# A mixture-of-experts tail on one core: TensorE reads and checks the next block's expert number one block ahead, behind the row transposes

## The reference, cut to what matters

```python
routing_weights, selected = jax.lax.top_k(probs, TOP_K)          # TOP_K = 2
routing_weights = routing_weights / routing_weights.sum(-1, keepdims=True)
gup = einsum(xf, gate_up_proj) + SCALING * (low-rank part)       # 512 -> 2 x 256, per expert
gates, h = jnp.split(gup, 2, axis=-1)
h = jax.nn.silu(gates) * h
out = einsum(h, down_proj) + SCALING * (low-rank part)           # 256 -> 512
y = einsum('tkh,tk->th', out_sel, routing_weights)
x = x + gb * y
```

## Time and profile before

| what | value |
|---|---|
| median of the runs | 1005.18 us |
| lowest and highest run | 1003.49 and 1005.67 us |
| the profiled execution's own time | 1002.81 us |
| its span, first to last instruction | 1001.1 us |
| mean granted clock of TensorE | 0.959 |
| busy: PE | 881.9 us (88%) |
| busy: DVE | 661.0 us (66%) |
| busy: ACT | 647.9 us (65%) |
| busy: POOL | 349.8 us (35%) |

### The profile page before, as it was taken

The page is one execution under the profiler, slowest core; times in us unless marked ns, Lnnn a source line. Parts: engine busy times, 40 slices in busy tenths (PEclk is TensorE's granted clock), DMA queues, the critical chain, the costliest instruction groups (busy, mean ns, idle before and its releaser), DMA issues.

```text
span 1001.1 us, 16358 instructions
## 1 busy us (share of the span) xinstructions
PE 881.9 (88%) x5127; PEld 532.6 (53%) x5127; DVE 661.0 (66%) x2299; ACT 647.9 (65%) x1416; POOL 349.8 (35%) x285
## 2 busy tenths in 40 slices
PE   7798998999999989999899999987469999999995
PEld 3456566565665765656657656464124444444442
DVE  3688989889889898898898887976322222222221
ACT  2767888888888888898888888874023333333331
POOL 2223344453454444534444434422102222222222
PEclk8999999999999999999999999977679999999998
DMA  9755327244153261442633513382524444443430
GB/s 334 252 149 159 107 85 191 57 134 147 56 180 106 87 191 47 145 131 71 180 88 104 159 44 106 96 341 96 214 74 85 76 77 83 75 78 73 84 48 0
DMA packets 59092, 120.43 MB, mean 120 GB/s; under 512 B 6896, under 2 KB 8560, under 8 KB 57984
## 3 DMA queue, kind: packets, MB, share of 16 engines
q1 hardware_dynamic: 50688, 102.28, 33.2%
q0 software_dynamic: 8176, 16.85, 9.0%
q10 hardware_dynamic: 144, 0.26, 0.1%
HBM read 51.94 MB, written 69.27 MB: 121 GB/s over the span
## 4 chain that ended last, share of the span: by engine, by line
PE 59%; DVE 16%; DMA 7%; POOL 7%; issue 6%; ACT 4%; SPq 0%; POOLq 0%; DVEq 0%; ACTq 0%
PE bank L714 15%; PE bank L110 11%; PE bank L116 8%; PE bank L727 7%; DMA xs_scratch<-t_arena 5%; POOL xs_scratch L1814 2%; POOL t_small L1801 2%; PE bank L487 1%; PE bank L549 1%; PE bank L498 1%; PE bank L559 1%; PE bank L503 1%; PE bank L529 1%; PE bank L467 1%; PE bank L536 1%
## 5 line engine op out<-in xcount | busy, mean ns | idle before, releaser
L110 PEld LDWEIGHTS bank<-t_arena 128*128 128x128 bf16 (+1 forms) x1536 | 123.5, 122 | 83.6 <-issue 15.9
L714 PE MATMUL bank<-t_arena 128*128 x312 | 145.9, 611 | 19.0 <-issue 17.5
L110 PE MATMUL bank<-t_arena 128*128 128x128 bf16 (+1 forms) x1536 | 152.7, 236 | 8.7 <-DVE t_arena L860 2.3
L116 PE MATMUL bank<-t_ident,t_arena 128*128 128x128 f32 x618 | 102.6, 285 | 41.5 <-DMA t_arena<-xs_scratch 8.4
L1840 POOL DMA_INDIRECT out_x<-t_arena,t_tokx x39 | 60.6, 1553 | 208.6 <-DVE t_small L1367 197.2
L116 PEld LDWEIGHTS bank<-t_ident,t_arena 128*128 128x128 f32 x618 | 72.4, 143 | 98.7 <-issue 40.4
L1372 DVE TENSOR_TENSOR t_arena<-t_arena,bank 128x256 f32<-128x256 f32 x39 | 16.4, 421 | 144.9 <-ACT t_arena L1722 144.9
L1722 ACT ACTIVATE t_arena<-bank 128x256 f32<-128x256 f32 x39 | 15.0, 384 | 148.7 <-PE bank L714 148.7
L714 PEld LDWEIGHTS bank<-t_arena 128*128 128x128 f32 x312 | 56.7, 192 | 85.3 <-issue 85.3
L727 PE MATMUL bank<-t_arena 128*128 x156 | 73.5, 593 | 0.5 <-ACT t_arena L1717 0.5
L1729 ACT ACTIVATE t_arena<-bank,t_small 128x128 f32<-128x128 f32 x156 | 58.7, 456 | 15.7 <-PE bank L116 13.7
(11 more groups left out here) (510 smaller groups left out, 2189.3 us busy)
## 6 DMA issues: line engine op xcount, KB each, us to landing
xs_scratch<-t_arena SPq DMA_DIRECT2D x16, 2064.0 KB, 11.6
wm_scratch<-t_arena SPq DMA_DIRECT2D x48, 256.0 KB, 2.3
t_arena<-wm_scratch SPq DMA_DIRECT2D x8, 1536.0 KB, 12.4
t_arena<-xs_scratch SPq DMA_DIRECT2D x39, 258.0 KB, 2.7
t_arena<-in_gate_up SPq DMA_DIRECT2D x32, 256.0 KB, 3.6
t_arena<-in_wmod SPq DMA_DIRECT2D x6, 1024.0 KB, 11.3
t_arena<-in_down SPq DMA_DIRECT2D x16, 256.0 KB, 3.6
out_x<-t_arena SPq DMA_DIRECT2D x16, 256.0 KB, 2.0
```

The costliest lines, as they stand in the source:

```text
L110: mm = pe.matmul(bank[:, s], lhs[:, s], rhs[:, s], start=True, stop=True)
L116: mm = pe.transpose(bank[:, 128 * k:128 * k + 128], src[:, 128 * k:128 * k + 128], idn)
L714: mm = pe.matmul(AA[u % 2][:, :], xT[u % 2][:, 128 * k:128 * k + 128], w_e[:, bass.ds(which[u], 1), 512 * k:512 * k + 512], start=(k == 0) ...
```

## The change

The read of the expert number leaves the up step. It now stands behind the row transposes of the same turn, and it reads the number of block `v = t = b + 2`, whose up step comes one turn later. The wait for the table moves with it. Three expert numbers (`b`, `u` and `v`) are then held in registers at a time, where two were held before.

```diff
             for b in range(-2, NB):
                 u, t = b + 1, b + 2
+                v = t
                 if b >= 0:
                     pe.wait_ge(up_dve, nth(UP_DVE, b, "fs"))
                     turned(pe, B0, fs[b % 2], 2, ident[:, :]).then_inc(dn_pe, 1)
@@ in the up step of block u
                     if u >= 2:
                         pe.wait_ge(up_dve, nth(UP_DVE, u-2, "fs"))
                     if u == 0:
-                        pe.wait_ge(tab_dve, nth(TAB_DVE, 0, "eb"))
-                    if u == 0:
                         pe.wait_ge(s_e,16 * NE)
-                    which[u] = pe.value_load(ebu[0:1, u:u + 1], min_val=0, max_val=NE - 1)
                     for k in range(4):
                         mm = pe.matmul(AA[u % 2][:, :], xT[u % 2][:, 128 * k:128 * k + 128],
                                        w_e[:, bass.ds(which[u], 1), 512 * k:512 * k + 512], start=(k == 0), stop=(k == 3))
@@ behind the row transposes of block t
                     if t >= 1:
                         pe.wait_ge(tn_act, nth(TN_ACT, t-1, "xT"))
                     turned(pe, P0, xg[t % RING], 4, ident[:, :]).then_inc(tn_pe, 1)
+                if v < NB:
+                    if v == 0:
+                        pe.wait_ge(tab_dve, nth(TAB_DVE, 0, "eb"))
+                    which[v] = pe.value_load(ebu[0:1, v:v + 1], min_val=0, max_val=NE - 1)
                 if b >= 0:
                     pe.wait_ge(dn_act, nth(DN_ACT, b, "fT"))
```

## The result

| | before | changed |
|---|---|---|
| median of 4 runs | 1004.54 us | 977.12 us |
| lowest and highest | 1003.49, 1005.67 | 973.20, 979.38 |
| the profiled execution's own time | 1002.81 | 979.38 |

The ratio is 0.9743, with a 95% interval of 0.9716 to 0.9770. Of 1004.5 us that is 25.8 us saved (23.1 to 28.5); the two medians lie 27.4 apart. In two later comparisons the same kernel came to 0.9743 (0.9720 to 0.9765) and 0.9746 (0.9711 to 0.9780), with medians 25.2 and 24.4 apart.

A forecast was written before the change was run, and what follows sets the result against it. TensorE and its sequencer bound the loop, with the expert-number read stuck behind the wait for `xT`. Gains of 23.7, 0.65 and 0.65 make 25.0 us: 1005.2 - 25.0 = 980.2 us, range 977 to 983, wider 975.5 to 991.

The forecast's parts named there:

- counting starts: Experts' loop: 12 matmul records of 0.43 and 6 transposes of 0.11 make a stall-free turn of 5.82 us, against 6.46.
- The two limits: Up step's first weight load: `xT`'s end plus 0.14 allows 0.64 us earlier; TensorE's own next start allows 0.65.
- The lesser reading: Rival, experts' loop: only the idle time shown comes back, 39 x 0.39 = 15.2 us, giving 990.0 us; chance 0.04.
- Up step 0: First up step, partly at the lower clock level: gain between bounds 0.44 and 0.88 us, taken as 0.65.
- Up step 1: Second up step: from `xT`'s end to the weight load 0.79 us, less 0.14, a gain of 0.65 us.
- The other 37: Up steps 2 to 38: 0.64 us gained each, 23.7 us together.
- The cost of the added read: Behind the row transposes: the read takes 0.64 us of the sequencer, hidden by about 2.5 us of cover, costed at nothing.
- The base: Whole kernel: median of the runs before the change, 1005.2 us, from which the 25.0 us gain was subtracted.
- the narrow range: Whole kernel: the forecast's own range, 977 to 983 us, with chance 0.74 for the forecast.
- Value waits for the matmuls: Rival, moved read: its value comes only when the matmuls in front are done; no gain, 1005.2 us; chance 0.06.
- load waits until the array is empty: Rival, moved read: the load cannot start until TensorE is empty; 14 us slower, 1019 us; chance 0.04.
- Output transfers become the bound: Rival, serial output transfers: 6.1 us a block, 10 us of the gain lost, 990 us; chance 0.12.

The follow-up runs named there:

- Four reads: The changed kernel with four reads of the next expert number in place of one, at the new place, three unused: 977.80 us (one run).
- eight: The changed kernel with eight reads of the next expert number in place of one, at the new place, seven unused: 1042.12 us (one run).

## Why the prediction was right, step by step

- **Per turn.** Forecast 6.46 - 5.82 = 0.64 us by counting starts; the chain shows 5.82. The two limits that agreed within 0.01 (`xT` plus 0.14, and the array's own next start) both hold to 0.01 (841.90 and 841.89). The lesser reading, 39 x 0.39 = 15.2 us, was wrong for the reason given: a piece of "busy" time was stall.
- **The sum.** Forecast 25.0 us, measured in the trace 25.49. Up step 0: from the first `xT` to the second, 8.47 us before and 8.10 after, so 0.37 in place of 0.65, below even my lower bound of 0.44. The array ran 5.99 us at the mixed clock where it had run 5.46; the earlier start was spent at the lower level. Up step 1: 2.30 to 1.64, 0.66 as forecast. The other 37: 24.46 us, 0.66 each, and not 0.64. In this one execution of the kernel before a few turns had a longer stall (mostly 0.40 to 0.43 of "issue" and not 0.39, and 0.54 in the second full turn), and those went too.
- **The cost of the added read.** Nothing, as forecast. The cover was said to be about 2.5 us; the address steps are done at 843.3 and the weight load is at 845.76, which is 2.4. Four reads fit and eight did not. The prediction called the first load, at 0.49 us, the exception above half a microsecond; none of the 39 lasts that long (longest 0.492), which changes nothing in the sum.
- **The base.** The forecast of 980.2 us was 1005.2 - 25.0. The median before came to 1004.54 with one more run, 0.6 lower, and the medians lie 27.4 us apart, 2.4 more than forecast; together they make the 3 us between 980.2 and 977.12. The forecast gain of 25.0 lies within the interval (23.1 to 28.5). As the experts' part gained 25.5 us and no more, the other 1.9 of the 27.4 is the scatter of a few runs, and that the time still fell in the narrow range owes something to its size.
- **The rivals.** "Value waits for the matmuls" and "load waits until the array is empty" fell with the trace of the changed kernel (load at 842.4, with at least six of the eight records not yet begun) and with four reads. "Output transfers become the bound" did not come true here, and the longer landing that it was priced by did not show (4.8 us in the median, 5.0 at most, as before). But it was near: 5.82 us a turn, against the 5.66 to 5.83 that these transfers took. One step further, with the read moved and 0.86 us less on TensorE, it was true.

## What to carry to other kernels

Look for work that needs nothing of a wait but stands behind it in an in-order stream: register loads, bounds checks, address steps. They do not count as busy, and the idle time that they left here understated them (0.39 of 0.64 us), because the pipelined matmul in front and the uncovered weight load behind were counted as busy; count starts against the densest stretch of the same trace. Such an edit pays only while its engine is the bound: after it, ask for the cycle of the next serial resource before planning another saving on the same engine.

## What the runs showed that I had not expected

- Leaving out the bounds of a register read does not leave out the check: it moved to each use, four assertions of 18 ns in the up step and two in the down step, in place of one.
- The same idle piece of 1.93 us was followed by a granted clock of 0.81 in one turn and of 1.00 in another; of fifteen pauses between 1.7 and 2.6 us seven were followed by a lower clock. The pieces of 1.04 us in the kernel with two reads behind the wait were not: 7.10 us a turn, as the sum has it.
- The experts' part repeats within 0.1 us from execution to execution and from chip to chip, while whole times differ by several us.
- The serial output transfers took 5.0 us from issue to landing when they were the bound, and 4.8 when they were not.
